# Second layer's slots laid anew, and the shared expert's loads spread over a turn of tiles

## The reference, cut to what matters

```python
# _L1_xattn_ref: 16 heads of 64, 375 keys
scores = jnp.einsum('bhnd,bhmd->bhnm', qh, kh) * scale
attn = jax.nn.softmax(scores, axis=-1)
out = jnp.einsum('bhnm,bhmd->bhnd', attn, vh)
...
# _L1_ffn_ref: 64 experts, 8 for each row, and one shared expert
shared = jax.nn.silu(xf @ Ws_up) @ Ws_down
aff = xf @ centroids.T
_, idx = jax.lax.top_k(aff + expert_biases, TOP_K)
w = jax.nn.sigmoid(sel); w = w / (jnp.sum(w, axis=-1, keepdims=True) + 1e-08)
...
routed = jnp.einsum('etd,efd,te->td', h, W_down, cw)   # silu(x W_up[e]) W_down[e], weighted
x = x + tanh(g) * (shared + routed)
```

## Time and profile before

| | |
|---|---|
| time, median of 3 runs | 2442.97 us (2440.88 to 2444.8) |
| the profiled execution | 2444.95 us, its span 2443.1 us |
| PE busy over the span | 2339.0 us (96%) |
| DVE, ACT, POOL busy | 1540.5 (63%), 1541.3 (63%), 764.5 us (31%) |
| second layer, scores of the first to the last sequence | 825 to 1934 us |
| the experts' tiles | 2000 to 2390 us |
| results loaded back, summed and stored | 2355 to 2443 us |

### The profile page before, as it was taken

How to read it: one execution, slowest core, us unless ns; L and a number is a source line. 1 busy time by engine, 2 the same in 40 slices (tenths; PEclk the granted TensorE clock), 3 DMA queues, 4 the chain that set the end, 5 groups by cost and what they waited for, 6 DMA issues and landing times. The chain is left out here.

```text
span 2443.1 us, 62803 instructions
## 1 busy us (share of the span) xinstructions
PE 2339.0 (96%) x19918; PEld 1799.5 (74%) x19919; DVE 1540.5 (63%) x4805; ACT 1541.3 (63%) x4682; POOL 764.5 (31%) x1087
## 2 busy tenths in 40 slices
PE   7999999999999899999999999999999969999996
PEld 5787787787877467666676766766766658888985
DVE  4777777777775466666666666666666654444447
ACT  2777777777775365665655656556566537777770
POOL 2000000000000022433342343343233257777771
PEclk7999999999999999999999999999999989999998
DMA  5111111111110511110111111111111077777689
GB/s 162 33 50 48 38 48 50 38 48 45 43 43 16 162 34 31 53 53 27 53 53 35 45 53 47 33 53 51 29 53 49 26 223 218 214 220 224 205 274 378
DMA packets 152414, 217.46 MB, mean 89 GB/s; under 512 B 24824, under 2 KB 112938, under 8 KB 152146
## 3 DMA queue, kind: packets, MB, share of 16 engines
q1 hardware_dynamic: 121442, 147.26, 20.2%
q0 software_dynamic: 26544, 60.21, 7.4%
q10 hardware_dynamic: 4160, 6.55, 0.7%
HBM read 121.88 MB, written 100.42 MB: 91 GB/s over the span
## 5 line engine op out<-in xcount | busy, mean ns | idle before, releaser
L1456 ACT ACTIVATE wup<-bank,nmax 112x375 f32<-112x375 f32 x512 | 294.4, 585 | 81.7 <-DVE nmax L1560 80.5
L766 ACT ACTIVATE prob<-bank,nmax 112x375 f32<-112x375 f32 x512 | 291.8, 579 | 82.5 <-DVE nmax L844 78.5
L844 DVE TENSOR_REDUCE nmax<-bank 112x1 f32<-112x375 f32 x512 | 254.8, 539 | 68.9 <-PE bank L588 68.9
L1560 DVE TENSOR_REDUCE nmax<-bank 112x1 f32<-112x375 f32 x512 | 255.5, 541 | 56.4 <-PE bank L1257 55.2
L1884 POOL DMA_INDIRECT expert_rows<-rows,ids x248 | 237.7, 958 | 79.5 <-issue 55.3
L1462 ACT COPY pT<-bank 128x336 f32<-128x336 f32 x512 | 201.9, 453 | 72.0 <-PE bank L1264 69.6
L1020 POOL TENSOR_TENSOR stats<-stats,neg_half 112x1 f32<-112x1 f32 x64 | 35.2, 550 | 619.9 <-DVE stats L874 615.9
L1320 PE MATMUL bank<-wup,wk 128*128 128x375 f32 x512 | 211.1, 505 | 4.9 <-DVE wup L1633 3.6
L1849 POOL TENSOR_TENSOR stats<-stats,neg_half 112x1 f32<-112x1 f32 x64 | 35.8, 559 | 545.8 <-DVE stats L1591 543.6
L595 PE MATMUL bank<-ident,prob 112*128 112x112 f32 x1536 | 200.5, 264 | 6.3 <-ACT prob L766 1.3
L1264 PEld LDWEIGHTS bank<-ident,wup 112*128 112x128 f32 x1536 | 163.0, 142 | 56.8 <-issue 34.4
(11 more groups left out here) (293 smaller groups left out, 5230.2 us busy)
## 6 DMA issues: line engine op xcount, KB each, us to landing
xr<-expert_rows SPq DMA_DIRECT2D x274, 129.0 KB
wup<-expert_results SPq DMA_DIRECT2D x14, 1024.0 KB, 18.7
wdn<-expert_results SPq DMA_DIRECT2D x14, 1024.0 KB, 20.6
wdn<-in_L_ffn_W_down_dram SPq DMA_DIRECT2D x8, 1024.0 KB, 12.3
expert_rows<-nowhere SPq DMA_DIRECT2D x56, 129.0 KB, 2.7
x_and_h_in<-stage SPq DMA_DIRECT2D x32, 224.0 KB, 2.4
xt<-x_and_h_in SPq DMA_DIRECT2D x32, 224.0 KB
context_turned<-ctxT SPq DMA_DIRECT2D x32, 187.5 KB, 2.2
```

The source lines that it names most:

```text
L766: nc.scalar.activation(prob[:, n % RING, :NK], s_bank[r][:NQ, :NK], ACT.Exp, bias=nmax[:, r:r + 1], accum_out=rsum[:, par, h:h + 1]).then_ ...
L844: nc.vector.tensor_reduce(nmax[:, r:r + 1], s_bank[r][:NQ, :NK], AX, ALU.max, negate=True).then_inc(maxed, 1)
L1456: nc.scalar.activation(prob[:, n % RING, :NK], s_bank[r][:NQ, :NK], ACT.Exp, bias=nmax[:, r:r + 1], accum_out=rsum[:, par, n:n + 1]).then_ ...
L1560: nc.vector.tensor_reduce(nmax[:, r:r + 1], s_bank[r][:NQ, :NK], AX, ALU.max, negate=True).then_inc(maxed, 1)
```

## The change

The slots of the second layer: `v10` and `v12` change places, `r0` goes from slot 7 to 8, `k7` from 11 to 13, `rank` from 13 to 14, `k6` from 14 to 15. DVE's parts move with them: `norm_y` from 3 to 4, `weigh` from 11 to 12, the picks from 13 and 14 to 14 and 15, the two `inverse` from slots 6 and 11 to 4 and 14. POOL's scatters are spaced by five exponentials for four scatters instead of one for one.

The experts: SP no longer issues a turn's late load and both loads for the shared expert behind the turn's last tile. The late load follows tile 8 of the turn. The two loads of 256 KB become four of 128 KB, one for each group, behind tiles 10 and 14 (first group, one turn ahead) and behind tiles 2 and 6 (second group, in its own turn). Each group has its own semaphore for each of the two loads. The number of late loads and the bytes stay.

```diff
 ORDER_C = [
-    (1, "post", "va1", "dve"), (2, "own", "v11", "act"), (2, "post", "wo", "dve"), (2, "own", "v12", "act"),
-    (3, "pre", "k0", "dve"), (4, "own", "v10", "act"), (4, "pre", "k2", "dve"), (5, "post", "lnT", "act"),
-    (5, "pre", "k4", "dve"), (6, "pre", "k1", "act"), (6, "pre", "k3", "dve"), (7, "own", "r0", "act"),
+    (1, "post", "va1", "dve"), (2, "own", "v11", "act"), (2, "post", "wo", "dve"), (2, "own", "v10", "act"),
+    (3, "pre", "k0", "dve"), (3, "own", "v12", "act"), (4, "pre", "k2", "dve"), (5, "post", "lnT", "act"),
+    (5, "pre", "k4", "dve"), (6, "pre", "k1", "act"), (6, "pre", "k3", "dve"), (8, "own", "r0", "act"),
     (8, "post", "router", "dve"), (9, "pre", "k5", "act"), (9, "pre", "xT", "dve"), (10, "own", "va0", "dve"),
-    (11, "pre", "k7", "dve"), (11, "pre", "q0", "act"), (12, "pre", "v00", "dve"),
-    (12, "pre", "v01", "act"), (13, "pre", "v02", "act"), (13, "post", "rank", "dve"), (14, "pre", "q1", "act"),
-    (14, "pre", "k6", "dve"), (15, "own", "r1", "act"),
+    (11, "pre", "q0", "act"), (12, "pre", "v00", "dve"), (12, "pre", "v01", "act"), (13, "pre", "v02", "act"),
+    (13, "pre", "k7", "dve"), (14, "pre", "q1", "act"), (14, "post", "rank", "dve"), (15, "pre", "k6", "dve"),
+    (15, "own", "r1", "act"),
 ]
...
-                parts_y = [(2, moments_y), (3, norm_y), (9, choose), (11, sigmoids), (11, weigh),
-                           (13, lambda p: pick(p, range(0, 2))), (14, lambda p: pick(p, range(2, 6))), (14, lambda p: pick(p, range(6, 8))), (15, place_end)]
+                parts_y = [(2, moments_y), (4, norm_y), (9, choose), (11, sigmoids), (12, weigh),
+                           (14, lambda p: pick(p, range(0, 2))), (15, lambda p: pick(p, range(2, 6))), (15, lambda p: pick(p, range(6, 8))), (15, place_end)]
...
-                    for v, at in enumerate((6, 11)):
+                    for v, at in enumerate((4, 14)):
...
-                    pool.wait_ge(exped, H * (p + 2) + 4 + 4 * k // 4)
+                    pool.wait_ge(exped, H * (p + 2) + 4 + 5 * k // 4)
...
+        x1_here = [sem(f"x1_here{q}") for q in range(EACH_TURN)]
+        x2_here = [sem(f"x2_here{q}") for q in range(EACH_TURN)]
+        NORMED_AT, RESIDUAL_AT = (10, 2), (14, 6)
...
-                    if n % TURN == TURN - 1:
-                        g = n // TURN
-                        if g < N - LATE:
-                            load_late(LATE + g)
-                        if g < SHARED_TURNS:
-                            sp.dma_start(x1[:], x1_rows[:, g]).then_inc(x1_here, 16)
-                            sp.dma_start(x3[:, g * EACH_TURN * D:(g + 1) * EACH_TURN * D], x2_rows[:, g]).then_inc(x2_here, 16)
+                    g, at = divmod(n, TURN)
+                    if at == 8 and g < N - LATE:
+                        load_late(LATE + g)
+                    for q in range(EACH_TURN):
+                        t = g * EACH_TURN if q == 0 else (g - 1) * EACH_TURN + q
+                        if at == NORMED_AT[q] and 0 <= t < OWN:
+                            sp.dma_start(x1[:, q * D:(q + 1) * D], x1_rows[:, t]).then_inc(x1_here[q], 16)
+                        if at == RESIDUAL_AT[q] and 0 <= t < OWN:
+                            sp.dma_start(x3[:, t * D:(t + 1) * D], x2_rows[:, t]).then_inc(x2_here[q], 16)
...
-                    pe.wait_ge(x1_here, m * 16)
+                    pe.wait_ge(x1_here[q], m * 16)
...
-                            dve.wait_ge(x2_here, m * 16)
+                            dve.wait_ge(x2_here[q], m * 16)
```

More of the change, by code:

```diff
@@ L1981, in expert_phase @@
         x3 = sb("x3_in", [P, OWN * D])
-        x2_here, x1_here, written = sem("x2_here"), sem("x1_here"), sem("written")
+        written = sem("written")
         EACH_TURN = 2
         SHARED_TURNS = OWN // EACH_TURN
+        x1_here = [sem(f"x1_here{q}") for q in range(EACH_TURN)]
+        x2_here = [sem(f"x2_here{q}") for q in range(EACH_TURN)]
+        NORMED_AT, RESIDUAL_AT = (10, 2), (14, 6)
         TURN_AT, COPY_AT, UP_AT, SILU_AT, DOWN_AT, ADD_AT = ((a, a + 7) for a in (0, 1, 2, 3, 5, 6))
@@ L2011, in expert_phase @@
         groups = "b q d -> (b q d)"
-        x2_rows, x1_rows = (d.rearrange(groups).rearrange("(p g r) -> p g r", p=P, r=EACH_TURN * D) for d in (x2_d, x1_d))
+        x2_rows, x1_rows = (d.rearrange(groups).rearrange("(p g r) -> p g r", p=P, r=D) for d in (x2_d, x1_d))
         out_rows = out.rearrange(groups).rearrange("(p g r) -> p g r", p=P, r=RUN)
```

## The result

The changed kernel takes 2415.6 us (median of 4 runs, 2413.25 to 2418.71) against 2443.89 (2440.88 to 2448.81) for the kernel before on the same chip: ratio 0.9885, interval 0.9869 to 0.9902. So it is faster, inside the range forecast, by 27 to 28 us where 20.5 were forecast.

What follows compares the result with a forecast made beforehand. PE bounds the second layer, POOL's scatters floor the experts' stage. 0.45 us in 30 sequences (13.5) plus 7.0 from the experts makes 20.5 us off 2444.95, on the median's scale 2423 us; range 2412 to 2434.

Steps and rivals of the forecast that it cites:

- The scores behind `r1`: Second layer: moving `rank` behind `q1` removes the scores' stall on ACT's fourth exponential, 0.20 us a sequence.
- `k7`, 0.25 us: Second layer: `k7` moved behind `v02` no longer waits for DVE to scale `va0`, 0.25 us a sequence.
- `k6`: Second layer, behind `rank`: lane free a tenth early, priced at nothing; rival: takes over `k7`'s wait, 0.25 us, chance 0.15.
- The other wait of the scores stays: Second layer, ahead of the third block of scores: this wait on ACT is unchanged, no gain.
- The experts: Experts' stage: spread loads end PE's stall for rows; POOL's 1.28 us scatters limit the gain to 7.0 us.
- I leave them: Experts' stage: three long POOL idles, 5.1 us, not at a turn's stall, stay and are taken off the 12.2.
- POOL without a floor: Rival, experts' stage: POOL sets no floor, PE's whole 19.7 us come back, 2411.8 or 2410 us; chance 0.08.
- Five holds for one: Rival, experts' stage: each of five spread issues stops PE instead of one, 2463.6 or 2461.5 us; chance 0.05.
- the experts give nothing: Rival, experts' stage: POOL idles as long as before, only the layer's 13.5 us won, 2431.5 or 2429.5; chance 0.09.

Runs made afterwards that it cites:

- rank_only: Kernel before with only `rank`, its picks and `k6` moved, `k7` left where it was: 2446.91 us, ratio 1.0016 to the kernel before.
- exp_first: Changed kernel with ACT's second group of exponentials in each four slots ahead of the copies of turned probabilities: 2412.13 us, ratio 0.9872 to the kernel before.
- pe_small: Changed kernel plus five unread 128x128 transposes on PE in each turn of 16 tiles, 0.55 us: 2417.62 us, ratio 0.9896 to the kernel before.
- pe_large: Changed kernel plus twelve unread 128x128 transposes on PE in each turn of 16 tiles, 1.32 us: 2431.57 us, ratio 0.9956 to the kernel before.
- loads_only: Kernel before with the changed kernel's expert phase (loads spread), second layer's slots as before: 2428.13 us, ratio 0.9941 to the kernel before.

## Why the prediction was right, and where it wasn't

- **The scores behind `r1`, 0.20 us: right.** Measured 0.21 (0.68 to 0.47). The cause is confirmed by `rank_only`, where the same move took the same stall away. The margin: ACT's fourth exponential is read out at 1212.49, and the scores start at 1212.69; before they started 0.05 us behind it. That leaves 0.15, inside the 0.05 to 0.17 forecast.
- **`k7`, 0.25 us: right.** Its wait is gone, and from start to start that is 0.27 (the turnings that stood ahead of it 0.80 to 0.63, the product itself 0.73 to 0.63). The two terms together gave 0.43 a sequence for 0.45. Group by group, in medians of some twenty sequences, nothing else on PE moved by more than 0.02 us, so no other move shows in PE's list; whether these two need the others no run says. What the step left out is the second use of the move, above.
- **`k6`: right.** `place_in` ends at 1211.42 and `k6` starts at 1211.57; less the 0.05 that a product takes to start, a tenth is left, as forecast. That rival fell, by a margin no larger than stated.
- **The other wait of the scores stays: right,** and `exp_first` shows that it was some 0.11 us and to be had.
- **The experts: the mechanism right, the size wrong.** PE's stall for rows went from 19.3 us to 2.7, the five loads cost PE nothing, POOL is the floor, and results lie for several tiles (that of tile 113 is ready at 2131.74 and scattered at 2136.33). The step that failed is "I leave them": three long idles of POOL, 5.1 us, were to stay because they don't lie at a turn's stall. They went, and with them all of the 12.2 us.

Here is one of them in the kernel before, first ACT's results, then POOL's scatters:

```profile
2156.79 0.48 ACT L2252 ACTIVATE wk<-bank,xr 128x256 f32<-128x256 f32 x1
2157.98 0.47 ACT L2252 ACTIVATE wk<-bank,xr 128x256 f32<-128x256 f32 x1
```

```profile
2158.46 0.97 POOL L2083 DMA_INDIRECT expert_results<-wk,dest  x1 [0.30 <-ACT wk L2252]
2161.80 0.97 POOL L2083 DMA_INDIRECT expert_results<-wk,dest  x1 [2.37 <-ACT wk L2252]
2163.07 0.98 POOL L2083 DMA_INDIRECT expert_results<-wk,dest  x1 [0.30 <-issue]
```

The scatter at 2161.80 writes the result that ACT had ready at 2158.45 (that of tile 113), so the wait named in brackets isn't what it stood for. In the records of POOL's sequencer the wait for this result stands at 2158.48, right behind it. The next record, a register move, comes only at 2161.59, 3.11 us later, where neighbours come about 1.3 us apart. The result that this next record asks for had been ready since 2159.90. The same pause, of 2.13 us at tile 56 and 3.11 at tiles 113 and 219, stands in the profiles of all runs, that of the changed kernel included. But there POOL has results lying ready and its sequencer runs ahead of the scatters: the move of tile 113 comes 0.17 us, that of tile 219 2.18 us before the previous scatter starts. The pause is still there, and the queued scatters cover it, but for 0.13 us at tile 56.

I had read the three idles as a cost of their own, to be taken off the 12.2 us. They were hardly that even before. The results came every 1.31 us (336.6 us for 257), and a scatter can follow the one before by 1.28, so POOL makes up a delay. At tile 113 a scatter starts 3.35 us behind its result, at tile 175 it is 1.08 again; only what was lost at tile 219 isn't all made up by tile 258. An estimate from these records: if each scatter starts 1.28 us behind the one before or 0.77 us behind its result, whichever is later, and 2.37, 3.35 and 3.35 us behind it at the three tiles, the 257 steps take 341.2 us, as measured; with 0.77 at these tiles too, 339.9. So the pauses were worth 1.3 us, and the other 10.9 are PE delivering results later than POOL could scatter them.

Where POOL is the floor and results don't lie long enough, the pauses do cost: that is what `pe_small` pays at tiles 56 and 113. `pe_large`, where the backlog is gone, has long idles at 56, 113 and 219 again.

- **The rivals.** POOL without a floor fell: 1.280 us a step under full pressure. That this step is made by busy DMA engines is unlikely: in the second layer of the changed kernel, at a DMA share of 0.16, POOL's scatters of 112 rows never follow each other by less than 1.24 us. Five holds for one fell: `PEld` waits for rows 5 times in the stage, 18 times before. That the experts give nothing fell with `loads_only`: 28 transfers more, each behind other work, made the kernel 0.6% faster. The Trainium skill, "DMA: Bandwidth & Descriptors", section "Anatomy of one DMA — SWDGE (gpsimd) path", which calls descriptor generation "small, variable", doesn't describe this stage: POOL's 0.98 us and the 0.30 behind it are what bounds it. The coalescing rule of the same page's "Rules for kernel authors" speaks for keeping the loads of two groups whole. Split and spread at once they gained; split alone they weren't run.
- **The rest of the difference.** 20.5 were forecast; the experts gave 5.2 more and the layer 1.0 less, which makes 24.7; the two short stretches around them show 0.9 more. The medians show 26.6 and 28.3. What is left is of the size by which the start of the second layer moves from one execution to the next; no run attributes it to the change.

## What to carry to other kernels

An idle of an engine that doesn't set the pace can't be taken as a cost by adding up its length: three idles of 5.1 us were worth 1.3, since the engine made them up behind. Ask who sets the pace after the change, and whether the engine will have a backlog at that place; if it will, count the idle as won. When an instruction is moved to take a stall away, look at the place that it leaves as well, since it was cover for its neighbours; `rank` moved alone made the kernel slower. And a small unread addition to the engine in question tells the floor from the follower in two runs: nearly free below the floor of another engine, paid in full above it. Its place counts too, since it is free inside any wait.

## What the runs showed of the hardware

POOL's sequencer stops for 2.13 us at one and 3.11 us at two fixed instructions of a long unrolled list of scatters (tiles 56, 113 and 219 of 288) in every profile, of kernels whose lists differ in other parts. (At tile 56 of `pe_large` the next result comes too late for the length to be read; the scatter stands 2.37 us behind its result there as elsewhere.) In the kernel before, at tile 113, the result asked for next is ready 1.7 us before the stop ends, so it isn't the wait for it. What the sequencer does in this time no run shows; a longer or shorter list, which would move the places, wasn't tried. A scatter of 128 rows of 256 float32 costs POOL 1.28 us from start to start, however long its inputs have been ready.
